# Two transposes per batch taken from TensorE, done in 32x32 squares by VectorE with a trip through DRAM

## The chip, the cores and the metric

The kernel runs on one core of one Trainium2 chip. The metric is the device time of one execution in microseconds: 476.37 us is the median of three runs (476.28, 476.37 and 478.12).

## The reference, cut to what matters

There are 8 batch entries (B = 8) of 512 rows (T) by 256 channels (D), all float32. For each entry:

```python
emb  = layernorm(x) + ctx                       # T x D
q, k, v = emb @ wq + bq, emb @ wk + bk, emb @ wv + bv
ek   = exp(k - max_over_rows(k));  ew = exp(w - max_of_row(w))   # w: T x T, a band 64 wide on each side, 0 outside
attn = (sigmoid(q) * (ew @ (ek * v)) / (ew @ ek)) @ wo + bo
a    = layernorm(attn + emb) * gamma + beta
x1   = x + tanh(g_xattn) * (layernorm(relu(a @ w1 + b1) @ w2 + b2 + a) * gamma + beta)    # hidden width 1024
xn   = layernorm(x1);  xp = xn shifted down by one row
r    = sigmoid((mu_r*xn + (1-mu_r)*xp) @ W_r.T);  kk = relu((mu_k*xn + (1-mu_k)*xp) @ W_k.T) ** 2
out  = x1 + tanh(g_ffn) * r * (kk @ W_v.T)
```

## The kernel before, in words

Every matrix product is made as three: each operand is split in a high part (rounded to TensorE's fp32r type, by ScalarE) and a low part (the rest, a subtraction on VectorE or GpSimd), and high*high, high*low and low*high are added. So almost every stage is: TensorE writes PSUM, ScalarE makes `*_hi`, VectorE or GpSimd makes `*_lo`, TensorE reads both.

Some values lie with rows on the partitions ("row form") and some with channels on the partitions ("channel form"). To turn a 512x256 array from one into the other, TensorE multiplies eight 128x128 tiles by the identity (`turn`, `turn_back`). Per entry this happens four times: the embedding (`turn_emb`), the exponentials of the keys (`turn_keys`, from `ek_t`, which is the buffer `y`, into PSUM pair 0), the normalised attention output (`turn(2, norm, mid_turned)`) and the last layer norm (`turn_fin`, from `norm` into PSUM pair 2). What follows the keys' turn is `ek_high` (ScalarE), `keys_low` and `weigh_values` (VectorE, ek * v, which gives `res`), `ev_high` (ScalarE) and `ev_low` (GpSimd). What follows the last norm's turn is `turned_copy` (ScalarE, into `xn_t`), `delta_of` (GpSimd, the difference to the row before), `mix_k` and `mix_r` (VectorE), their splits, and the products `ffn_k` and `ffn_r`.

The order on each engine is written out by hand. A prologue treats entry 0; then `step(i, p)` runs for i = 1 to 7 on every engine, and an epilogue finishes entries 6 and 7. A step works on several entries at once: i is in attention and its first hidden layers, b = i-1 in the second hidden layers and the two norms behind them, a = i-2 in the gated product at the end, d = i+1 has its keys, queries and values made, and e = i+2 is loaded. Engines wait for each other by semaphores only. TensorE's step begins with `weigh(i, 0, ...)` (ew @ ek), then `turn_emb(d)`, `weigh(i, 1, ...)` (ew @ (ek*v)) with `add_hidden(b, 1)` inside, `ffn_k(a)`, `keys(d)`, and ends with `turn(2, norm, mid_turned)`, `queries(d)`, `hidden(i, 0)`, `hidden(i, 1)`, `values(d)`, `turn_keys(d)`, `add_hidden(i, 0)`, `turn_fin(b)`. SyncE issues the DMAs of a step in the order x again, x, ctx, store.

Names in rows: PSUM is `ps`; the keys' and the ek*v parts are `ek_hi`, `ek_lo`, `ev_hi`, `ev_lo`; the buffer `res` also holds the values; `y` holds the keys' exponentials or the attention's quotient. Buffers are shared, so `ek_lo<-y,ek_hi` (line 225) on GpSimd is `y_low`, the low part of the quotient, `hid_lo<-xr,hid_hi` is `xr_low`, and `ev_lo<-xk,ev_hi` is `sq_low`.

## Time and profile before

| | |
|---|---|
| median of 3 runs | 476.37 us |
| the profiled execution's own time | 477.9 us |
| its span, first to last instruction | 476.2 us |
| TensorE busy | 453.5 us (95%), 3080 matmuls |
| VectorE busy | 391.8 us (82%), 733 instructions |
| ScalarE busy | 239.6 us (50%) |
| GpSimd busy | 259.4 us (54%) |
| DMA | 23.35 MB, 49 GB/s on average |
| granted TensorE clock, mean | 0.996 |

The span is cut in 40 slices on the page. TensorE stands at 9 tenths (90% or more) in nearly every one behind the first ten; its clock is at 9 tenths of full speed or more in all. The repeated step is read best in a stretch between two turns of the same kind. In a row of the timeline the first number is the start, the second the time from the first to the last of the merged instructions, and the bracket is idle time of the engine ahead of them with what ended it.

### The profile page before, as it was taken

How to read it: one execution, taken by the hardware profiler on the slowest of the kernel's cores; microseconds unless marked ns; L12 is line 12 of the kernel's file. 1: busy time of each engine (PE TensorE's matmuls, PEld its weight loads, DVE VectorE, ACT ScalarE, POOL GpSimd, SP SyncE). 2: the span in 40 equal slices, each digit the busy share in tenths (PEclk: the TensorE clock that was granted, in tenths of full speed). 3: DMA queues.
4: the chain of work that ended last, by engine and by line, in shares of the span. 5: the costliest groups of instructions: out<-in, count | busy, mean ns of one | idle time of the engine just before them, and what ended most of it. 6: DMA issues, size and time to landing. Idle time of an engine off the chain costs nothing.

```text
span 476.2 us, 8229 instructions
## 1 busy us (share of the span) xinstructions
PE 453.5 (95%) x3080; PEld 412.4 (87%) x3080; DVE 391.8 (82%) x733; ACT 239.6 (50%) x372; POOL 259.4 (54%) x239
## 2 busy tenths in 40 slices
PE   7889989899999999999999999999999999999975
PEld 7779788779989898999989898899989898897975
DVE  4898879986959989598968989599867979489987
ACT  3582562645265634736356643735345543538253
POOL 2574843661587535971577634973567335953621
PEclk9999999989999999999999999999999999999999
DMA  8740410102001300022001210021000110011002
GB/s 265 267 132 8 144 50 2 44 12 79 1 1 63 114 3 0 1 89 89 1 1 45 94 41 1 1 89 44 1 2 0 51 39 1 1 45 45 2 0 89
DMA packets 21895, 23.35 MB, mean 49 GB/s; under 512 B 992, under 2 KB 20960, under 8 KB 21856
## 3 DMA queue, kind: packets, MB, share of 16 engines
q1 hardware_dynamic: 20768, 21.26, 13.7%
q10 hardware_dynamic: 1088, 1.57, 1.0%
q8 instruction: 24, 0.39, 0.3%
q14 instruction: 15, 0.12, 0.1%
...
## 4 chain that ended last, share of the span: by engine, by line
PE 43%; issue 19%; POOL 16%; DVE 14%; ACT 4%; DMA 2%; ACTq 0%; POOLq 0%; DVEq 0%
PE ps L1361 40%; DVE y L670 4%; POOL xk_lo L225 3%; POOL hid_lo L225 3%; PE ps L1367 2%; POOL a_rows L434 2%; DMA hid<-in_wo 2%; DVE xk L738 1%; PE ps L1376 1%; POOL emb L434 1%; POOL ek_lo L225 1%; POOL ev_lo L225 1%; POOL x_beta L434 1%; DVE y L667 1%; DVE hid_lo L814 1%
## 5 line engine op out<-in xcount | busy, mean ns | idle before, releaser
L1361 PE MATMUL ps<-w_hi,hid_hi 128*128 128x256 f32 x288 | 72.2, 288 | 0.8 <-issue 0.5
L1361 PE MATMUL ps<-w_lo,hid_hi 128*128 128x256 f32 x288 | 70.6, 281 | 0.0
L814 DVE SCALAR_TENSOR_TENSOR hid_lo<-ps,neg_b,hid 128x512 fp32r<-128x512 f32 x60 | 41.3, 739 | 34.5 <-ACT hid L1190 34.5
L1361 PEld LDWEIGHTS ps<-w_hi,hid_hi 128*128 128x128 f32 x288 | 54.2, 188 | 3.5 <-DVE y L677 2.2
L1361 PEld LDWEIGHTS ps<-w_lo,hid_hi 128*128 128x128 f32 x288 | 54.3, 189 | 0.1
L670 DVE RECIPROCAL y<-y 128x512 f32<-128x512 f32 x16 | 53.7, 3353 | 0.6
L1361 PE MATMUL ps<-a_hi,w_hi 128*128 128x512 f32 x128 | 50.8, 397 | 1.1 <-DVE hid_lo L814 1.1
L1361 PE MATMUL ps<-a_hi,w_lo 128*128 128x512 f32 x128 | 50.7, 396 | 0.0
L1184 ACT ACTIVATE hid_hi<-ps,b 128x512 fp32r<-128x512 f32 x60 | 37.9, 686 | 24.8 <-PE ps L1361 24.8
L225 POOL TENSOR_TENSOR ev_lo<-res,ev_hi 128x1024 fp32r<-128x1024 f32 x8 | 19.1, 2383 | 51.7 <-ACT ev_hi L1129 51.7
L1361 PE MATMUL ps<-w_hi,hid_lo 128*128 128x256 f32 x288 | 41.6, 284 | 3.4 <-DVE hid_lo L814 2.2
L1361 PEld LDWEIGHTS ps<-w_hi,hid_lo 128*128 128x128 f32 x288 | 37.1, 188 | 4.8 <-DVE hid_lo L814 2.4
L1190 ACT ACTIVATE hid<-hid_hi,neg_b 128x512 f32<-128x512 f32 x60 | 40.1, 725 | 0.0
L1361 PE MATMUL ps<-a_lo,w_hi 128*128 128x512 f32 x128 | 35.1, 396 | 0.0
L434 POOL TENSOR_TENSOR a_rows<-norm,gamma_rows 128x1024 f32<-128x1024 f32 x8 | 20.1, 2509 | 19.7 <-issue 17.3
L1361 PEld LDWEIGHTS ps<-a_hi,w_hi 128*128 128x128 f32 x128 | 24.0, 188 | 6.7 <-DVE hid_lo L814 1.6
L225 POOL TENSOR_TENSOR xk_lo<-xk,xk_hi 128x1024 fp32r<-128x1024 f32 x7 | 17.2, 2460 | 22.6 <-ACT xk_hi L1141 22.6
L1361 PEld LDWEIGHTS ps<-a_lo,w_hi 128*128 128x128 f32 x128 | 24.1, 188 | 5.8
L1361 PEld LDWEIGHTS ps<-a_hi,w_lo 128*128 128x128 f32 x128 | 24.1, 189 | 5.2
L1361 PE MATMUL ps<-emb_hi,w_hi 128*128 128x512 f32 x64 | 26.9, 420 | 0.5 <-ACT emb_hi L1099 0.5
L1361 PE MATMUL ps<-emb_hi,w_lo 128*128 128x512 f32 x64 | 25.6, 399 | 0.0
L225 POOL TENSOR_TENSOR hid_lo<-xr,hid_hi 128x1024 fp32r<-128x1024 f32 x5 | 12.1, 2410 | 22.5 <-ACT hid_hi L1148 22.5
...
## 6 DMA issues: line engine op xcount, KB each, us to landing
x_in<-in_x SPq DMA_DIRECT2D x8, 512.0 KB, 4.4
emb<-in_ctx SPq DMA_DIRECT2D x8, 512.0 KB, 3.5
x_beta<-in_x SPq DMA_DIRECT2D x8, 512.0 KB, 3.6
out<-out_sb SPq DMA_DIRECT2D x7, 512.0 KB, 2.9
hid<-in_w SPq DMA_DIRECT2D x2, 512.0 KB, 6.8
x<-in_pos ACTq DMA_DIRECT2D x1, 512.0 KB, 6.2
out_sb<-in_pos ACTq DMA_DIRECT2D x1, 512.0 KB, 7.1
x<-in_w SPq DMA_DIRECT2D x1, 512.0 KB, 4.0
```

What stands on the lines that cost most here:

```text
L225: eng.tensor_tensor(dst, src, f32(hi), ALU.subtract).then_inc(done, 1)
L434: pool.tensor_tensor(dst.rearrange("p (a d) -> p a d", a=TT), src.rearrange("p (a d) -> p a d", a=TT), r, op).then_inc(done, 1)
L667: dve.scalar_tensor_tensor(out=tile(y, c, T), in0=tile(gate_q, c, T), scalar=1.0, in1=bank(1, c), op0=ALU.add, op1=ALU.mult).then_inc(den_ ...
L670: dve.reciprocal(tile(y, c, T), tile(y, c, T)).then_inc(recip_done, 1)
L738: dve.scalar_tensor_tensor(out=tile(dst, c, T), in0=tile(out_sb, c, T), scalar=vec[:, mu + c:mu + c + 1], in1=xn_t[:, c * (T + 1):c * (T + ...
L814: dve.scalar_tensor_tensor(out=tile(lo, b, T), in0=bank(relu_pair(n, q), b), scalar=neg_b1[:, m:m + 1], in1=tile(shifted, b, T), op0=ALU.m ...
L1184: act.activation(tile(hi, b, T), bank(relu_pair(n, q), b), ACT.Relu, bias=b1[:, m:m + 1]).then_inc(hid_hi_done, 1)
L1190: act.activation(tile(shifted, b, T), f32(tile(hi, b, T)), ACT.Identity, bias=neg_b1[:, m:m + 1]).then_inc(hid_shifted, 1)
L1361: return pe.matmul(o, s, m, start=start, stop=stop, skip_group_check=True)
L1367: last = pe.transpose(bank(dst, c)[:, a * P:(a + 1) * P], src[:, D * a + c * P:D * a + (c + 1) * P], ident)
L1376: last = pe.transpose(tile(pair(dst), a)[:, c * P:(c + 1) * P], src[:, T * c + a * P:T * c + (a + 1) * P], ident)
```

## The change

From entry 2 on (`FIRST_EK`) the keys, and for entries 0 to 5 the last norm, are no longer turned by TensorE. VectorE turns each 32x32 square in place among its own 32 partitions (`dve.transpose`, `turn_key_squares`, `turn_fin_squares`, two instructions of 128x512 each) into a blocks buffer (`norm` for the keys, `hid[0]` for the norm). SyncE then stores this buffer to DRAM in one DMA of 512 KB (`room`), waits for it, and reads it back in four DMAs of 128 KB, each to 32 partitions (`spread`), into `y` for the keys and `hid[1]` for the norm. The squares land in another order of columns, so the readers use views (`by_squares`, `by_columns`). The keys' low part goes from VectorE (`keys_low`) to GpSimd (`ek_low`, between the `ff` and the `fin` statistics). The values' weighing reads `y` in SBUF in place of PSUM. `recip` is cut in `gate_den` and `recip`. Orders: on TensorE `turn_emb` goes one entry ahead, to where `turn_keys` was, and `keys(d)` comes ahead of `ffn_k(a)`; on ScalarE `turned_copy` goes to the next step behind `sums_high(i, 1)`, `ek_high` comes ahead of `hidden_high(i, 0)`; on VectorE `hidden_low(i, 1)` moves behind `normalise_fin`, the squares and `keep_values`, and `emb_low` moves ahead of the first `gate_den`.

VectorE, the end of step 4, before (`res<-ps,bv_rows` is `keep_values`, `ek_lo` is `keys_low`, `res<-ps,res` is `weigh_values`; `hid_lo` x4 is both `hidden_low(i, 0)` and `(i, 1)`):

```order
L572 BN_STATS st_fin<-x 128x6 x4
L580 MEMSET held 128x1
L582 BN_AGGR mv_fin<-st_fin 128x2 x4
L814 SCALAR_TENSOR_TENSOR hid_lo<-ps,neg_b,hid 128x512 x4
L719 TENSOR_SCALAR norm<-x,rs_fin,nmr_fin 128x256 x3
L618 TENSOR_TENSOR res<-ps,bv_rows 128x1024
L637 TENSOR_TENSOR ek_lo<-ps,ek_hi 128x1024
L642 TENSOR_TENSOR res<-ps,res 128x1024
```

and now:

```order
L636 BN_STATS st_fin<-x 128x6 x4
L644 MEMSET held 128x1
L646 BN_AGGR mv_fin<-st_fin 128x2 x4
L903 SCALAR_TENSOR_TENSOR hid_lo<-ps,neg_b,hid 128x512 x2
L806 TENSOR_SCALAR norm<-x,rs_fin,nmr_fin 128x256 x3
L725 STREAM_TRANSPOSE hid<-norm 128x4x128 x2
L682 TENSOR_TENSOR res<-ps,bv_rows 128x1024
L903 SCALAR_TENSOR_TENSOR hid_lo<-ps,neg_b,hid 128x512 x2
L710 TENSOR_TENSOR res<-y,res 128x1024
```

`keys_low` has left, two square transposes stand behind the norm, and `hidden_low(i, 1)` comes later.

VectorE, the middle of step 5, ahead of the attention's sum (`res<-ps,emb`), before:

```order
L572 BN_STATS st_head<-x_in 128x6 x4
L580 MEMSET held 128x1
L582 BN_AGGR mv_head<-st_head 128x2 x4
L814 SCALAR_TENSOR_TENSOR hid_lo<-ps,neg_b,hid 128x512 x2
L626 TENSOR_REDUCE ek_sums<-y 128x4 x2
L630 COPY ek_rows<-ek_sums 128x6x4
L774 TENSOR_TENSOR res<-ps,emb 128x1024
```

and now:

```order
L636 BN_STATS st_head<-x_in 128x6 x4
L644 MEMSET held 128x1
L646 BN_AGGR mv_head<-st_head 128x2 x4
L718 STREAM_TRANSPOSE norm<-y 128x16x32 x2
L690 TENSOR_REDUCE ek_sums<-y 128x4 x2
L694 COPY ek_rows<-ek_sums 128x6x4
L903 SCALAR_TENSOR_TENSOR hid_lo<-ps,neg_b,hid 128x512 x2
L863 TENSOR_TENSOR res<-ps,emb 128x1024
```

The two square transposes of the keys read `y` and write `norm`; the keys' row sums come ahead of the low part of the hidden layer.

GpSimd, the end of step 4, before:

```order
L429 TENSOR_TENSOR nmr_ff<-nm_ff,rs_ff 128x4
L419 TENSOR_TENSOR ve_fin<-mv_fin,eps_col 128x4
L420 TENSOR_TENSOR nm_fin<-mv_fin,minus_one 128x4
L427 TENSOR_TENSOR rs_fin<-ve_fin,minus_half 128x4
L429 TENSOR_TENSOR nmr_fin<-nm_fin,rs_fin 128x4
L225 TENSOR_TENSOR ev_lo<-res,ev_hi 128x1024
```

and now:

```order
L490 TENSOR_TENSOR nmr_ff<-nm_ff,rs_ff 128x4
L231 TENSOR_TENSOR ek_lo<-y,ek_hi 128x1024
L480 TENSOR_TENSOR ve_fin<-mv_fin,eps_col 128x4
L481 TENSOR_TENSOR nm_fin<-mv_fin,minus_one 128x4
L488 TENSOR_TENSOR rs_fin<-ve_fin,minus_half 128x4
L490 TENSOR_TENSOR nmr_fin<-nm_fin,rs_fin 128x4
L231 TENSOR_TENSOR ev_lo<-res,ev_hi 128x1024
```

The keys' low part stands between the statistics `ff` and `fin` of entry b; the row `ev_lo<-res,ev_hi` is the first of the next step.

The diff, cut:

```diff
+SQ = 32
+NB = P // SQ
+FIRST_EK = 2
...
+        ek_blocks, ek_square = norm, y
+        fin_blocks, fin_square = hid[0], hid[1]
+        def by_squares(ap):
+            return ap.rearrange("p (a x j) -> p x a j", a=NB, j=SQ)
+        def by_columns(ap):
+            return ap.rearrange("p (x a j) -> p x a j", a=NB, j=SQ)
...
+        def ek_low(eng, n):
+            low(eng, by_columns(ek_lo), by_squares(ek_square), by_columns(ek_hi), ek_hi_done, n + 1, ek_lo_done)
...
+            def spread(square, blocks, room, filled, free, free_count, landed):
+                sp.dma_start(room.rearrange("(p n) -> p n", p=P), blocks).then_inc(room_filled, 16)
+                sp.wait_ge(room_filled, 16 * filled)
+                sp.wait_ge(free, free_count)
+                for b in range(NB):
+                    sp.dma_start(square[SQ * b:SQ * (b + 1)].rearrange("i (a n) -> i a n", a=NB),
+                                 room.rearrange("(a i b n) -> b i a n", a=NB, i=SQ, b=NB)[b]).then_inc(landed, 16)
+            def spread_keys(n):
+                sp.wait_ge(ek_turned, FIRST_EK + DC * (n + 1 - FIRST_EK))
+                after(sp, ek_landed, keys_moved(n - 1))
+                spread(ek_square, ek_blocks, rooms[0], keys_room(n), ek_summed, DC * (n + 1), ek_landed)
+            def spread_fin(n):
+                sp.wait_ge(fin_turned, DC * (n + 1))
+                after(sp, fin_landed, fin_moved(n - 1))
+                spread(fin_square, fin_blocks, rooms[1], fin_room(n), hid_lo_done, 2 * (NQ * (n + 1) + 2), fin_landed)
...
                     load_x(i + 2)
+                if has(i + 1):
+                    spread_keys(i + 1)
+                if has(i + 2):
                     load_ctx(i + 2, p)
                 if has(i - 2):
                     store(i - 2)
+                if not is_last(i):
+                    spread_fin(i - 1)
...
                 stats("ff", b)
+                if has(d):
+                    pool.wait_ge(x1_done, TT * (b + 1))
+                    ek_low(pool, d)
                 stats("fin", b)
...
             def weigh_values(n):
                 dve.wait_ge(val_done, n + 1)
-                dve.tensor_tensor(val, pair(0), val, ALU.mult).then_inc(ev_done, 1)
+                if n < FIRST_EK:
+                    dve.tensor_tensor(val, pair(0), val, ALU.mult).then_inc(ev_done, 1)
+                else:
+                    dve.wait_ge(ek_landed, keys_moved(n))
+                    dve.tensor_tensor(by_columns(val), by_squares(ek_square), by_columns(val), ALU.mult).then_inc(ev_done, 1)
+            def turn_key_squares(n):
+                dve.wait_ge(mid_turned, 1)
+                dve.wait_ge(a_scaled_done, 1)
+                dve.wait_ge(ek_done, DC * (n + 1))
+                for c in range(DC):
+                    dve.transpose(ek_blocks.rearrange("p (b x c i) -> p c b x i", b=NB, x=TT, c=DC)[:, c],
+                                  tile(ek_t, c, T).rearrange("p (x b i) -> p b x i", x=TT, b=NB)).then_inc(ek_turned, 1)
+            def turn_fin_squares(n):
+                dve.wait_ge(norm_done["fin"], TT * (n + 1))
+                for c in range(DC):
+                    dve.transpose(fin_blocks.rearrange("p (b c x j) -> p c b x j", b=NB, x=TT, c=DC)[:, c],
+                                  norm.rearrange("p (x c b i) -> p c b x i", c=DC, x=TT, b=NB)[:, c]).then_inc(fin_turned, 1)
...
-            def recip(n, c):
+            def gate_den(n, c):
                 dve.wait_ge(den_done, DC * n + c + 1)
                 dve.wait_ge(exp_q_done, DC * n + c + 1)
-                if c == 0:
+                if c == 0 and n < FIRST_EK:
                     dve.wait_ge(ek_turned, n + 1)
                 dve.scalar_tensor_tensor(out=tile(y, c, T), in0=tile(gate_q, c, T), scalar=1.0, in1=bank(1, c),
                                          op0=ALU.add, op1=ALU.mult).then_inc(den_read, 1)
+            def recip(n, c):
                 dve.wait_ge(den_read, DC * n + c + 1)
                 dve.reciprocal(tile(y, c, T), tile(y, c, T)).then_inc(recip_done, 1)
...
@@ -723,6 +810,8 @@
                 after(dve, fin_turned, DC * (n - 1))
                 dve.wait_ge(nmr_done["mid"], n + 1)
+                if n > 0 and has(n + 1):
+                    dve.wait_ge(room_filled, 16 * keys_room(n + 1))
                 normalise_tiles("mid", res, range(TT - FIRST_DVE, TT))
...
             def step(i, p):
                 a, b, d, e = i - 2, i - 1, i + 1, i + 2
                 sums_low(i, 0)
+                if has(d) and d > FIRST_EK:
+                    emb_low(d)
+                gate_den(i, 0)
                 recip(i, 0)
                 sums_low(i, 1)
+                gate_den(i, 1)
+                if d == FIRST_EK:
+                    emb_low(d)
                 if has(a):
                     mix_k(a)
-                if has(d):
-                    emb_low(d)
                 recip(i, 1)
                 if has(a):
...
                 if has(e):
                     head_stats(e)
+                if has(d):
+                    turn_key_squares(d)
+                    sum_keys(d)
                 hidden_low(b, 2)
-                if has(d):
-                    sum_keys(d)
                 attention_sum(i, p)
                 hidden_low(b, 3)
...
                 finish_x1(b)
                 fin_stats(b)
                 hidden_low(i, 0)
-                hidden_low(i, 1)
-                normalise_fin(b)
+                if not is_last(i):
+                    normalise_fin(b)
+                    turn_fin_squares(b)
                 if has(d):
                     keep_values(d)
-                    keys_low(d)
+                hidden_low(i, 1)
+                if is_last(i):
+                    normalise_fin(b)
+                if has(d):
                     weigh_values(d)
...
             def ek_high(n):
-                act.wait_ge(ek_turned, n + 1)
+                if n < FIRST_EK:
+                    act.wait_ge(ek_turned, n + 1)
+                    act.activation(ek_hi, pair(0), ACT.Copy).then_inc(ek_hi_done, 1)
+                else:
+                    act.wait_ge(ek_landed, keys_moved(n))
+                    act.activation(by_columns(ek_hi), by_squares(ek_square), ACT.Copy).then_inc(ek_hi_done, 1)
...
@@ -1132,8 +1238,14 @@
                 after(act, xr_done, DC * n)
                 for c in range(DC):
                     o = c * (T + 1) + 1
-                    act.wait_ge(fin_turned, DC * n + c + 1)
-                    act.activation(xn_t[:, o:o + T], bank(2, c), ACT.Copy).then_inc(xn_t_done, 1)
+                    if n == BATCH - 2:
+                        act.wait_ge(fin_turned, DC * n + c + 1)
+                        act.activation(xn_t[:, o:o + T], bank(2, c), ACT.Copy).then_inc(xn_t_done, 1)
+                    else:
+                        act.wait_ge(fin_landed, fin_moved(n))
+                        act.activation(by_columns(xn_t[:, o:o + T]),
+                                       fin_square.rearrange("p (a c x j) -> p c x a j", a=NB, c=DC, j=SQ)[:, c], ACT.Copy
+                                       ).then_inc(xn_t_done, 1)
...
             def step(i, p):
                 a, b, d, e = i - 2, i - 1, i + 1, i + 2
-                if has(d):
-                    after(act, v_done, d)
+                if d == FIRST_EK:
+                    act.wait_ge(v_done, d)
                     emb_high(d)
                 if has(a):
+                    turned_copy(a)
                     mixed_high(a)
                     mixed_r_high(a)
                     relu_k(a)
...
                 if has(d):
                     exp_q(d)
+                    ek_high(d)
                 hidden_high(i, 0)
                 hidden_high(i, 1)
                 normalise("fin", b, x1)
-                if has(d):
-                    ek_high(d)
-                if not is_last(i):
-                    turned_copy(b)
+                if has(e):
+                    act.wait_ge(v_done, e)
+                    emb_high(e)
                 if has(d):
                     sums_high(d, 0)
                     ev_high(d)
@@ -1443,7 +1556,10 @@
...
             def turn_emb(n, p):
                 pe.wait_ge(emb_done, n + 1)
-                after(pe, ev_done, n)
+                if n <= FIRST_EK:
+                    after(pe, ev_done, n)
+                else:
+                    relus_read(NQ * (n - 2) + 1)
...
                 if part == 0:
                     pe.wait_ge(lo_ready, n + 1)
                     near(dst, 0, lo, (ew_hi,))
-                    after(pe, xn_t_done, DC * (n - 1))
                     relus_read(NQ * (n - 1) + 2)
...
                 pe.wait_ge(ek_hi_done, i + 1)
                 pe.wait_ge(val_done, i + 1)
                 weigh(i, 0, 1, ek_hi, ek_lo, ek_lo_done, den_done)
-                if has(d):
+                if d == FIRST_EK:
                     turn_emb(d, 1 - p)
                 pe.wait_ge(ev_hi_done, i + 1)
                 pe.wait_ge(sums_lo_done, 2 * i + 1)
                 weigh(i, 1, 2, ev_hi, ev_lo, ev_lo_done, num_done, lambda: add_hidden(b, 1))
+                if has(d):
+                    keys(d)
                 if has(a):
                     if a == 0:
                         for u in (6, 7):
                             pe.wait_ge(w_lo_done[u], 1)
                     ffn_k(a)
-                if has(d):
...
                 hidden(i, 1)
                 if has(d):
                     values(d)
-                    turn_keys(d)
+                if has(e):
+                    turn_emb(e, p)
                 if not is_last(i):
                     add_hidden(i, 0)
-                    turn_fin(b)
```

## Rows read from the trace of the kernel before

**Rows 1.** Table of stretches: length, busy (instructions) of PE, PEld, DVE, ACT, POOL, clock, DMA.

```profile
207.60:262.00 54.40, 54.18 (x372) 49.48 (x371) 45.46 (x88) 28.11 (x43) 32.47 (x28) 1.00 0.12 40
```

**Rows 2.** Chain of waits, two steps: start, us, engine, output and line.

```profile
207.58 0.87 PE ps L1367 x8
...
219.76 0.87 PE ps L1376 x8
...
223.50 0.87 PE ps L1367 x8
...
262.03 0.87 PE ps L1367 x8
```

**Rows 3.** Timeline of PE, `weigh(4, 1)`, the first product that reads `ev_lo`.

```profile
229.88 0.63 PE L1361 MATMUL ps<-ev_lo,tile_rows 128*68 128x256 f32 x4
```

**Rows 4.** Timeline of POOL, end of step 3 and step 4.

```profile
218.12 0.20 POOL L419 TENSOR_TENSOR ve_fin<-mv_fin,eps_col 128x4 f32<-128x4 f32 x1 [3.40 <-DVE mv_fin L582]
...
219.64 0.20 POOL L429 TENSOR_TENSOR nmr_fin<-nm_fin,rs_fin 128x4 f32<-128x4 f32 x1
227.40 2.38 POOL L225 TENSOR_TENSOR ev_lo<-res,ev_hi 128x1024 fp32r<-128x1024 f32 x1 [7.56 <-ACT ev_hi L1129]
229.73 2.04 POOL L259 TENSOR_TENSOR out_sb<-xn_t 128x512 f32<-128x512 f32 x2
...
245.97 2.39 POOL L225 TENSOR_TENSOR ek_lo<-y,ek_hi 128x1024 fp32r<-128x1024 f32 x1
...
250.00 2.40 POOL L225 TENSOR_TENSOR ev_lo<-xk,ev_hi 128x1024 fp32r<-128x1024 f32 x1
```

**Rows 5.** Timeline of DVE, the same stretch.

```profile
214.49 1.71 DVE L696 SCALAR_TENSOR_TENSOR x<-x,rs_ff,x_beta 128x256 f32<-128x256 f32 x4 [0.52 <-POOL rs_ff L427]
...
220.57 1.05 DVE L719 TENSOR_SCALAR norm<-x,rs_fin,nmr_fin 128x256 f32<-128x256 f32 x3
...
223.80 1.22 DVE L642 TENSOR_TENSOR res<-ps,res 128x1024 f32<-128x1024 f32 x1
...
232.17 1.42 DVE L738 SCALAR_TENSOR_TENSOR xk<-out_sb,vec,xn_t 128x512 f32<-128x512 f32 x2
...
238.74 1.32 DVE L738 SCALAR_TENSOR_TENSOR xr<-out_sb,vec,xn_t 128x512 f32<-128x512 f32 x2
...
251.59 1.41 DVE L814 SCALAR_TENSOR_TENSOR hid_lo<-ps,neg_b,hid 128x512 fp32r<-128x512 f32 x2 [4.92 <-ACT hid L1190]
...
254.72 1.21 DVE L774 TENSOR_TENSOR res<-ps,emb 128x1024 f32<-128x1024 f32 x1
```

**Rows 6.** Timeline of ACT, the same stretch.

```profile
226.27 1.05 ACT L1129 ACTIVATE ev_hi<-res 128x1024 fp32r<-128x1024 f32 x1
...
248.46 1.26 ACT L1105 ACTIVATE y<-ps,kbias 128x512 f32<-128x512 f32 x2 [2.48 <-POOL ek_lo L225]
```

**Rows 7.** Timeline of DVE, end of step 1.

```profile
103.65 1.71 DVE L696 SCALAR_TENSOR_TENSOR x<-x,rs_ff,x_beta 128x256 f32<-128x256 f32 x4
...
114.56 1.21 DVE L642 TENSOR_TENSOR res<-ps,res 128x1024 f32<-128x1024 f32 x1
```

**Rows 8.** Timeline of DVE and POOL where both ran at once, in two places.

```profile
81.09 2.40 POOL L225 TENSOR_TENSOR ek_lo<-y,ek_hi 128x1024 fp32r<-128x1024 f32 x1 [7.49 <-ACT ek_hi L1166]
...
81.65 2.93 DVE L653 TENSOR_TENSOR w_lo<-x,w_hi 128x1024 fp32r<-128x1024 f32 x1
```

```profile
434.18 2.41 POOL L434 TENSOR_TENSOR x_beta<-x_beta,beta_t 128x1024 f32<-128x1024 f32 x1
...
434.91 2.47 DVE L719 TENSOR_SCALAR norm<-x,rs_fin,nmr_fin 128x256 f32<-128x256 f32 x3
```

**Rows 9.** Groups by line: the reciprocal; busy, mean ns, idle before.

```profile
L670 DVE RECIPROCAL y<-y 128x512 f32<-128x512 f32 x16 | 53.7, 3353 | 0.6
```

**Rows 10.** DMA issues by line: engine, count, KB each, us to landing.

```profile
emb<-in_ctx SPq DMA_DIRECT2D x8, 512.0 KB, 3.5
...
out<-out_sb SPq DMA_DIRECT2D x7, 512.0 KB, 2.9
```

More of the change, by code:

```diff
@@ L200, in flamingo_gated_block @@
         gated_done, out_done = sem("gated_done"), sem("out_done")
+        ek_landed, fin_landed = sem("ek_landed"), sem("fin_landed")
+        room_filled = sem("room_filled")
+        rooms = [nc.dram_tensor(f"room{k}", [P * PAIR], F32, kind="Internal").ap() for k in range(2)]
         last_norm_dve, last_sq_lo = sem("last_norm_dve"), sem("last_sq_lo")
@@ L1082, in normalise @@
                 act.wait_ge(nmr_done[kind], n + 1)
+                if kind == "mid" and n > 0 and has(n + 1):
+                    act.wait_ge(room_filled, 16 * keys_room(n + 1))
                 for a in range(FIN_DVE if kind == "fin" else 0, TT - FIRST_DVE if kind == "mid" else TT):
@@ L1709, in step @@
                     ffn_k(a)
-                if has(d):
-                    keys(d)
                 if is_last(i):
```

13 lines of the change are left out of this document (11 added, 2 removed).

## The prediction

> **What bounds the kernel now.** I read the table of stretches first: in a stretch of 54.40 us TensorE is busy for 54.18, VectorE for 45.46, GpSimd for 32.47 [rows 1]. The chain of waits gives the period: the turn behind the middle norm stands at 207.58 and again at 262.03, so a step takes 54.45 us, and each turn of eight tiles is 0.87 us of the path [rows 2]. TensorE sets the pace. Then I looked how far the others are behind, because TensorE gives way only as far as they let it. GpSimd ends `ev_lo` at 227.40 + 2.38 = 229.78, and TensorE takes it up at 229.88 [rows 3, 4]: 0.1 us of slack. VectorE's only long idle time in a step is 4.92 us, ahead of `hidden_low(b, 2)` [rows 5]. So the kernel is at two bounds at once, TensorE's work and a ring of VectorE, ScalarE and GpSimd.
>
> **What TensorE saves.** Steps 1 to 6 lose one `turn_keys` and one `turn_fin` each: 12 x 0.87 = 10.4 us [rows 2]. `turn_emb` only moves. If TensorE alone decided, that would be the gain.
>
> **The ring behind the change.** I follow it from w, the end of `weigh_values`, to the next w. Before, w = 223.80 + 1.22 = 225.02, and it comes back after 54.45.
>
> 1. w to `ev_lo`. `ev_high` is 1.05 [rows 6], `ev_low` 2.38 [rows 4], with hand-overs w + 3.55. Before it took 4.76, since `ev_high` stood behind `sums_high`.
> 2. `turned_copy(a)` now stands behind `sums_high(i, 1)`, which needs four products that read `ev_lo`. I take 1.6 for these, the copy of the sums and the first half of `turned_copy`: 0.5 for the products (merged row 0.63, rows 3), two times half of a 1.05 copy [rows 6]. `delta_of` takes 2.04 [rows 4]; `mix_k` reads its result: w + 7.2. `mix_k` 1.42 [rows 5]: w + 8.65. Until then VectorE does `emb_low`, both gate products and the first reciprocal, which hides them. The second reciprocal 3.35 [rows 9], `mix_r` 1.32: w + 13.3. Before, `mix_r` ended at 238.74 + 1.32 = 240.06, w + 15.04 [rows 5].
> 3. From there to `exp_keys` the same chain as before: 248.46 - 240.06 = 8.4 [rows 5, 6], w + 21.7.
> 4. `exp_keys` 1.26 [rows 6]. Then the two squares of the keys, 1.35 (below), the row sums and their copy, 254.72 - 253.00 = 1.7, `hidden_low(b, 2)` 1.41 [rows 5]: the attention's sum starts at w + 27.45. Before: 254.72, w + 29.7. The squares use up part of the 4.92 of idle time.
> 5. From the attention's sum to the end of `finish_x1`: 214.49 + 1.71 + 54.45 - 254.72 = 15.9, unchanged: w + 43.4.
> 6. From there to the next w. Before 225.02 - 216.20 = 8.8. Now GpSimd does `ek_low` first, 2.4 as for any 128x1024 row of its kind, and VectorE's statistics (1.9, ended by 218.12) hide only part of it. The four small operations 219.84 - 218.12 = 1.7 [rows 4], the norm's three tiles 1.05, squares 1.35, `keep_values` 1.22 (priced as `weigh_values`), `hidden_low(i, 1)` 1.41, `weigh_values` 1.22, less 0.3 for overlapping neighbours [rows 5]: 10.25. `keys_low` (1.2) has left; the squares and the wait for GpSimd eat more than that.
>
> Sum 43.4 + 10.25 = 53.65, against 54.45: 0.8 us per step, not the 1.74 that TensorE would allow. TensorE will wait about 1.1 us per step for `ev_lo`, and for `val_done` some tenths.
>
> **The sum.** In step 1 the stretch from `finish_x1` to w was 115.77 - 105.36 = 10.4 [rows 7], already as long as the new 10.25, so w stays at 115.6. In step 2 `ev_high` still stands behind `sums_high`; I add 0.95 for that. The last changed end is that of step 6: 115.6 + 0.95 + 5 x 53.65 = 384.8, `ev_lo` at 388.35. Before, TensorE took it at 229.88 + 3 x 54.45 = 393.23. The gain is 4.9 us. Step 7 and the epilogue have the same work. The profiled execution took 477.9 (span 476.2), so it would take 473.0; the median of the runs lies 1.5 lower, at 476.37, and I forecast 471.5.
>
> **What the trace doesn't show.** A square transpose. The lower end is a plain instruction of the same size, half of 1.32, so 0.66 [rows 5]; the upper end is the slowest of that size, 3.35 [rows 9]. I take 0.67: the data moves once, nothing is iterated. Each further 0.1 costs 0.1 x 4 x 5 = 2 us in all, since all four of a step lie on the ring. At the upper end the kernel would take 54 us more; I give that no weight worth a range. Views with a column order of 32 in ScalarE's, GpSimd's and VectorE's readers: between no cost and, for five instructions of 1 to 2.4 us, a doubling of some; I take nothing.
>
> The trip through DRAM. A store of 512 KB lands in 2.9, a load of 512 KB in 3.5 [rows 10]: 6.4 as the lower end; one load after another, 2.9 + 4 x 3.5 = 16.9 as the upper. The four are issued without a wait between, so I add 1.2 for their issues: 7.6. For the norm the time from the squares' end (w - 3.65) to `turned_copy` (w + 4.6) is 8.25: hidden, with 0.6 to spare, and every microsecond beyond that is one more per step. At the upper end it would be 8.6 x 5 = 43 us. The keys have 15 us, from w + 24.35 to `ek_high` near w + 40: hidden. Behind the norm's trip on SyncE's queue wait the next `load_again` and `load_x`; their data is wanted 14 us later. Behind the keys' trip waits `load_ctx`, which before went out right after the attention's sum; it is wanted by GpSimd 9 us later and lands in 3.5.
>
> **Ports.** At 81.65 a VectorE instruction with two SBUF inputs took 2.93 us; a GpSimd one ran from 81.09 to 83.49, and the first ended 1.1 after it. At 434.91 three norm tiles took 2.47 in place of 1.05, beside GpSimd's 434.18 to 436.59 [rows 5, 8]. So some VectorE instructions wait until GpSimd's is done. `weigh_values` now has two SBUF inputs, but GpSimd is idle there; `mix_k` has two, and I have let it start only behind `delta_of`. Whether a square transpose waits no row shows. The Trainium skill (SBUF — State Buffer, Who interferes with whom) says that a VectorE instruction with at most one SBUF input and outside the two-port modes does not contend with GpSimd, and names `tensor_scalar`, which the second pair of rows shows waiting, among those that do. By that rule the trace agrees for both pairs, and the transposes would not wait.
>
> **The rivals.** *TensorE decides alone* (all 10.4 us are gained): 466.0. For it: the ring is only 0.8 us shorter by sums of rows, and an error of 0.2 on each of six hand-overs would open it. Against it: `ev_lo` was already just in time [rows 3, 4] and `ek_low` now delays the statistics.
>
> *The trip or the views take the gain away*: the norm lands 1 us late per step, 5 x 1.0 = 5, giving 476.5. For it: a DMA that waits in SyncE's queue for `hid_lo_done` and issues four parts has only 0.6 to spare. Against it: DMA is lightly loaded, busy for 0.12 [rows 1].
>
> *The squares cost more than a plain instruction*: place, the four of VectorE on the ring; price, 20 us in all per microsecond of one. It decides for slower from 0.67 + (4.9 + 2.4) / 20 = 1.03 us on. At twice the plain time, 0.67 more, it gives 471.5 + 13.4 = 485. Nothing in the rows speaks for it but the reciprocal, which has the same shape and takes 5 times as long.
>
> The Trainium skill (VectorE: DVE Perf Modes, The three transpose paths) gives VectorE 311 ns for a 128x128 block of bf16 and in its rules names TensorE for full tiles; eight such blocks would be an estimate of 2.5 us where I have 1.35, and the time by that 483. No row here shows it, and the page's figure holds the fixed part of one small instruction.
>
> *The keys' squares wait for GpSimd*, as `tensor_scalar` does in rows 8. `y_low` ends at w + 21.7 as before at 248.36, the head's statistics last until 250.00, and there `sq_low` takes 2.40 [rows 4]: from w + 23.4 to 25.8. The second square would start at 23.7 and wait 2.1. Five steps: 10.5 more, 482.
>
> **How the numbers follow.** Less than 0.5% (2.4 us) cannot be told from no change. The forecast, the ring at about 53.65 per step: 0.46, with its own range 468.5 to 474.0. TensorE alone: 0.13. The trip or the views: 0.17. Dear squares: 0.12. Squares that wait: 0.12. Faster: 0.46 + 0.13 = 0.59; same: 0.17; slower: 0.24. The range reaches from a little below TensorE's bound, 465.5, to 482, where the waiting squares lie; the dear ones are left out.
>
> **What will show it.** In the profile after: a turn of the middle norm every 53.6 to 53.7 us; TensorE idle for about 1 us per step ahead of the product that reads `ev_lo`; two squares in 1.3 to 1.4 us, at both places; the ring's stretch from `finish_x1` to w 10.2 long; ScalarE's `turned_copy` started by `sums_high` and not by a DMA. I am wrong if `turned_copy` waits for the landing, if a square takes over 1 us, if VectorE waits for something new inside the ring, or if the period is 52.7 (TensorE alone).

## The result: slower by 1.4%, where a gain of 1% was forecast

| | before | after |
|---|---|---|
| median | 476.32 us (4 runs, 475.46 to 478.12) | 483.07 us (4 runs, 481.24 to 486.18) |
| ratio, 95% interval | | 1.014 (1.008 to 1.021) |
| the profiled execution's own time, span | 477.9, 476.2 us | 481.24, 479.5 us |
| TensorE, VectorE, GpSimd busy | 453.5, 391.8, 259.4 us | 444.7, 402.6, 273.0 us |
| DMA | 23.35 MB | 35.95 MB |

The forecast was 471.5. The runs after are also further apart than those before, and their times follow the clock: granted clocks of 0.996, 0.991, 0.988 and 0.984 go with 481.24, 481.9, 484.24 and 486.18 us. Of the six runs of e2 below, the three that were over 1.5% above its fastest (489.05 to 490.7 us, clocks of 0.983 to 0.988) count as slow and are left out of its numbers.

The page of the changed kernel shows that the change did what it says. TensorE has 96 instructions fewer and 8.8 us less to do, and the trips are there (engine, times, KB each, us to landing):

```profile
PE 444.7 (93%) x2984; PEld 402.6 (84%) x2984; DVE 402.6 (84%) x751; ACT 238.9 (50%) x372; POOL 273.0 (57%) x245
...
room<-norm SPq DMA_DIRECT2D x6, 512.0 KB, 2.7
y<-room SPq DMA_DIRECT2D x24, 128.0 KB, 2.9
room<-hid SPq DMA_DIRECT2D x6, 512.0 KB, 2.7
hid<-room SPq DMA_DIRECT2D x24, 128.0 KB, 3.0
```

The table of stretches, each from one attention sum to the next, is the profile after's answer to [rows 1]:

```profile
142.66:198.63 55.97, 52.46 (x354) 47.88 (x354) 48.42 (x90) 30.14 (x48) 36.88 (x31) 1.00 0.25 80
198.63:254.33 55.70, 54.27 (x354) 49.33 (x354) 46.77 (x90) 25.85 (x40) 32.32 (x29) 0.97 0.22 72
254.33:310.30 55.97, 52.46 (x354) 47.88 (x354) 48.49 (x90) 30.14 (x48) 36.89 (x31) 1.00 0.26 81
310.30:364.60 54.30, 52.46 (x354) 47.88 (x354) 45.07 (x82) 24.90 (x38) 33.09 (x26) 1.00 0.20 64
```

TensorE's work per step is down from 54.18 to 52.46 us, as forecast. But the steps are not alike: 55.97, 55.70, 55.97, 54.30, where before each took 54.45 and the forecast had 53.65. Something costs 2.3 us in some steps and nothing in others. VectorE's timeline has it (in rows, L718 and L725 are the squares, L694 the copy that spreads the keys' row sums, L863 the attention's sum, L710 `weigh_values`):

```profile
168.16 1.22 DVE L710 TENSOR_TENSOR res<-y,res 128x1024 f32<-128x1024 f32 x1
...
194.97 2.43 DVE L694 COPY ek_rows<-ek_sums 128x24 f32<-128x24 f32 x1
...
198.63 1.21 DVE L863 TENSOR_TENSOR res<-ps,emb 128x1024 f32<-128x1024 f32 x1
...
208.88 1.29 DVE L792 TENSOR_TENSOR res<-ps,a_rows 128x512 f32<-128x512 f32 x2 [2.31 <-PE ps L1474]
...
215.73 0.87 DVE L783 SCALAR_TENSOR_TENSOR x<-x,rs_ff,x_beta 128x256 f32<-128x256 f32 x2
...
221.99 1.30 DVE L725 STREAM_TRANSPOSE hid<-norm 128x512 f32<-128x512 f32 x2
...
225.63 1.22 DVE L710 TENSOR_TENSOR res<-y,res 128x1024 f32<-128x1024 f32 x1
...
250.42 1.30 DVE L718 STREAM_TRANSPOSE norm<-y 128x512 f32<-128x512 f32 x2 [2.66 <-ACT y L1207]
251.65 1.24 DVE L690 TENSOR_REDUCE ek_sums<-y 128x4 f32<-128x512 f32 x2
252.92 0.18 DVE L694 COPY ek_rows<-ek_sums 128x24 f32<-128x24 f32 x1
253.01 1.40 DVE L903 SCALAR_TENSOR_TENSOR hid_lo<-ps,neg_b,hid 128x512 fp32r<-128x512 f32 x2
254.33 1.21 DVE L863 TENSOR_TENSOR res<-ps,emb 128x1024 f32<-128x1024 f32 x1
...
306.63 2.43 DVE L694 COPY ek_rows<-ek_sums 128x24 f32<-128x24 f32 x1
```

The same copy of 24 numbers per partition takes 2.43 us, then 0.18, then 2.43. GpSimd's timeline at the second and third of them:

```profile
250.56 2.42 POOL L231 TENSOR_TENSOR ev_lo<-xk,ev_hi 128x1024 fp32r<-128x1024 f32 x1
...
252.94 2.42 POOL L495 TENSOR_TENSOR a_rows<-a_rows,bias_rows 128x1024 f32<-128x1024 f32 x1
...
304.27 2.43 POOL L231 TENSOR_TENSOR ev_lo<-xk,ev_hi 128x1024 fp32r<-128x1024 f32 x1
...
306.64 2.39 POOL L495 TENSOR_TENSOR a_rows<-a_rows,bias_rows 128x1024 f32<-128x1024 f32 x1
```

The copy that starts at 306.63 comes while `sq_low` ends and `a_rows` begins; it is over when `a_rows` is, at 309.03. The one at 252.92 came 0.06 us before `sq_low`'s end and 0.02 before `a_rows`, and got through. The one at 141.25 got through as well (0.18 us), though it came 0.07 before `sq_low`'s end and 0.01 before `a_rows`, just like the one at 306.63: which of the two happens is decided below the hundredth of a microsecond that the profile prints. Behind the copy stands `hidden_low(b, 2)`, and TensorE's `ffn_v` waits for that:

```profile
198.86 0.36 PE L1474 MATMUL ps<-w_hi,ev_hi 128*128 128x256 f32 x1 [2.87 <-DVE hid_lo L903]
...
230.62 0.69 PE L1474 MATMUL ps<-ev_lo,tile_rows 128*68 128x256 f32 x4 [0.64 <-POOL ev_lo L231]
...
254.56 0.36 PE L1474 MATMUL ps<-w_hi,ev_hi 128*128 128x256 f32 x1 [0.59 <-DVE hid_lo L903]
...
310.53 0.36 PE L1474 MATMUL ps<-w_hi,ev_hi 128*128 128x256 f32 x1 [2.87 <-DVE hid_lo L903]
```

The first of the two waits of 2.87 us had a second cost. Stretches of the table (columns as above; the clock is the last number but two):

```profile
196.00:200.10 4.10, 1.24 (x8) 1.27 (x9) 4.07 (x5) 3.04 (x6) 3.69 (x2) 0.92 0.45 132
200.10:204.20 4.10, 4.10 (x26) 4.10 (x25) 3.55 (x12) 0.61 (x2) 1.57 (x4) 0.66 0.38 128
...
308.00:312.00 4.00, 1.47 (x12) 1.50 (x13) 3.96 (x6) 2.70 (x5) 3.36 (x2) 1.00 0.46 131
312.00:316.00 4.00, 4.00 (x36) 4.00 (x35) 3.96 (x12) 0.75 (x2) 1.57 (x4) 1.00 0.47 135
```

TensorE was busy for 1.24 of 4.10 us, and in the stretch behind it the granted clock averages 0.66, that is 1.2 GHz for about two thirds of it and 2.4 GHz for the rest. That makes 1.5 of the 2.0 us by which the step of 55.70 is longer than one of 53.7, although its own copy took only 0.18 us. TensorE's 354 instructions of that step take 54.27 us in place of 52.46, VectorE waits 2.31 us for `ff_sum` (`res<-ps,a_rows`, 208.88) where it waits 1.42 in the other steps, and from the attention's sum to the end of `finish_x1` it is 17.98 us in place of 16.47. Most of the rest, 0.4 us, is ScalarE's `turned_copy`, which waits in this step for the norm's trip to land:

```profile
232.13 1.16 ACT L1246 ACTIVATE xn_t<-hid 128x512 f32<-128x512 f32 x2 [0.40 <-DMA hid<-room]
```

Behind the second wait, as long and with TensorE busy for 1.47 of 4.00, the clock stayed at 2.4 GHz. The runs with lower mean clocks, above, are the longer ones.

### The profile page after: what moved, and what is told of

The parts are those of the page before. It is cut to its first block, busy times and chain, and to the rows that moved or that the text cites. A ratio compares the mean times of both kernels' runs of the same rounds, so it can differ in the third digit from the quotient of the medians.

```text
span 479.5 us, 8151 instructions
## 1 busy us (share of the span) xinstructions
PE 444.7 (93%) x2984; PEld 402.6 (84%) x2984; DVE 402.6 (84%) x751; ACT 238.9 (50%) x372; POOL 273.0 (57%) x245
## 2 busy tenths in 40 slices
DMA packets 30536, 35.95 MB, mean 75 GB/s; under 512 B 1952, under 2 KB 28064, under 8 KB 30496
## 4 chain that ended last, share of the span: by engine, by line
PE 30%; POOL 21%; DVE 20%; issue 20%; ACT 5%; DMA 2%; SPq 0%; DVEq 0%; POOLq 0%; ACTq 0%
PE ps L1474 28%; POOL ek_lo L231 4%; POOL xk_lo L231 3%; DVE y L757 3%; POOL hid_lo L231 2%; POOL emb L495 2%; POOL a_rows L495 2%; DVE hid_lo L903 2%; DVE xk L827 2%; PE ps L1480 2%; DVE emb_lo L654 2%; DVE y L751 1%; DVE ek_sums L690 1%; ACT y L1207 1%; POOL x_beta L495 1%
## 5 line engine op out<-in xcount | busy, mean ns | idle before, releaser
L1474 PEld LDWEIGHTS ps<-w_lo,hid_hi 128*128 128x128 f32 x288 | 54.4, 189 | 0.2
L757 DVE RECIPROCAL y<-y 128x512 f32<-128x512 f32 x16 | 53.5, 3347 | 0.3
L231 POOL TENSOR_TENSOR ek_lo<-y,ek_hi 128x1024 fp32r<-128x1024 f32 x13 | 31.2, 2400 | 16.6 <-DVE x L783 9.2
L1230 ACT ACTIVATE sums_r<-ps 68x256 fp32r<-68x256 f32 x16 | 6.1, 380 | 43.7 <-PE ps L1607 23.5
```

The lines of the kernel that those rows point to most:

```text
L231: eng.tensor_tensor(dst, src, f32(hi), ALU.subtract).then_inc(done, 1)
L757: dve.reciprocal(tile(y, c, T), tile(y, c, T)).then_inc(recip_done, 1)
L1230: act.activation(sums_r[part][0:FAR], bank(2, part, D)[0:FAR], ACT.Copy).then_inc(sums_hi_done, 1)
L1474: return pe.matmul(o, s, m, start=start, stop=stop, skip_group_check=True)
```

## The experiments

Theory: the copy waits for GpSimd's running instruction, and the 2.4 us of that wait, together with what stands behind it, turn a gain into a loss. Rivals: moving the data through DRAM, or the new orders, cost it. In each batch of runs, before ran on the same chip (476.83, 476.78 and 476.62 us); the changed kernel as it stands was measured only with the result above, where before took 476.32.

**e1: the copy as a reduction.** The same numbers in the same place, as a `tensor_reduce` over an axis of length 1.

```diff
-dve.tensor_copy(ek_rows..., ek_sums...)
+dve.tensor_reduce(ek_rows..., ek_sums... (last axis of length 1), AX_X, ALU.add)
```

> The changed kernel, with the small copy of the keys' row sums (ek_rows, 128x24) made by a tensor_reduce over an axis of length one in place of tensor_copy. Theory (the copy waits until a GpSimd instruction is done, 2.43 us in place of 0.18 in steps 3 and 5, and TensorE's ffn_v behind it): no copy above 0.4 us, TensorE's wait ahead of ffn_v 0.6 us in every step in place of 2.87 in two, the ring at 54.2 us per step, 474.5 us, and less scatter. Rival (the trips through DRAM and the longer ring make the loss, the two waits are hidden by others): within 1 us of the changed kernel's 481 to 486.

Measured 472.69 us (472.16 to 474.44), ratio 0.992 (0.990 to 0.994). One instruction in another form takes 10.4 us off the changed kernel (483.07), and makes the change a gain of 0.8%. The theory held, and by more than it promised. Every such instruction takes 0.18 us, and the steps of the loop are alike:

```profile
142.20:195.91 53.71, 52.46 (x354) 47.88 (x354) 46.16 (x90) 27.87 (x44) 34.61 (x30) 1.00 0.26 79
195.91:249.65 53.74, 52.47 (x354) 47.89 (x354) 46.17 (x91) 27.89 (x44) 34.62 (x30) 1.00 0.25 79
249.65:303.37 53.72, 52.46 (x354) 47.88 (x354) 46.24 (x90) 27.88 (x44) 34.59 (x30) 1.00 0.25 79
```

**e10: the copy stays, GpSimd waits.** This tells the form of the instruction from the wait: `tensor_copy` in its place, and GpSimd's `a_rows` held back until it is done.

```diff
+                if has(d):
+                    pool.wait_ge(ek_rows_done, d + 1)
                 finish_a(b, 1 - p)
                 x_plus_beta(b)
```

> The changed kernel with tensor_copy kept in its form and its place; GpSimd alone is edited: it waits for the row sums' copy before it starts a_rows (and so x_beta behind it). Theory (the copy waits for whatever GpSimd instruction runs, and missed the gap between two of them by hundredths of a us): the copies of 2.43 us become 0.2 to 0.3, at most what is left of ev_lo, no TensorE wait of 2.87 ahead of ffn_v, time 472 to 475. Rival (the copy's form is dear by itself, whatever GpSimd does): copies stay at 1.8 to 2.4 us and the time at 481 or more.

Measured 473.62 (472.42 to 475.72), ratio 0.994 (0.992 to 0.997), as the theory had it. The timeline, VectorE and GpSimd together:

```profile
246.06 2.41 POOL L231 TENSOR_TENSOR ev_lo<-xk,ev_hi 128x1024 fp32r<-128x1024 f32 x1
...
248.42 0.18 DVE L696 COPY ek_rows<-ek_sums 128x24 f32<-128x24 f32 x1
...
248.68 2.39 POOL L495 TENSOR_TENSOR a_rows<-a_rows,bias_rows 128x1024 f32<-128x1024 f32 x1 [0.20 <-DVE ek_rows L696]
```

The copy takes 0.18 us in steps 1 to 6, and a step 53.71 to 53.73. So the form is not dear by itself; what costs is GpSimd's instruction beside it. This is the decisive run, since VectorE's program is untouched. Below I call this wait, of a VectorE instruction for the end of GpSimd's, the lock. Span against span the changed kernel loses 479.5 - 472.1 = 7.4 us to it. The attention's sums of the two kernels show where: 1.5 us by the first (a copy of 1.79), 0.3 by the second (1.3 given back), then 2.2, 2.0, 2.3 and 0.6 more.

**e2 and e6: the keys alone**, the last norm turned by TensorE as before, with `turned_copy` and VectorE's end of the step in their old places; e6 with the reduction.

```diff
-                    spread_fin(i - 1)
-                    turn_fin_squares(b)
+                    turn_fin(b)        # TensorE, with turned_copy from PSUM
```

> Only the keys turned in squares; the last norm is turned by TensorE as before, and VectorE's end of the step stands in the old order without keys_low. Theory (each part is paid in VectorE's ring): TensorE saves 5.2 us; the stretch from finish_x1 to the end of weigh_values is about 8 us, so the ring would allow 53 us, but the keys' squares and the copy's wait delay hidden_low(b, 2) and ffn_v behind it, in some steps by 2.4: 473 to 477 us. Rival (the norm's part is what loses, the keys' part gains): 471 or less.

> The keys-only half of the change (last norm turned by TensorE as before) with the row-sum copy as tensor_reduce. Theory (the two copies of 2.43 to 2.44 us and the two TensorE waits of 2.56 behind them made keys-only slow): those waits shrink to about 0.6, time 473 to 477, scatter between runs under 3 us. Rival (moving the keys through DRAM is what costs, by its trips or its place on the queues): 483 or more with no copy over 0.2 us.

Measured for e2 482.68 (479.61 to 483.32), ratio 1.010 (1.006 to 1.014). Both the theory and the rival missed. The theory had the copy's wait in it, but priced it too low: it is 2.43 us in two steps and 1.80 in an earlier one, and the clock comes on top. The copy waits in two steps one after the other, and TensorE with it:

```profile
196.60 2.44 DVE L692 COPY ek_rows<-ek_sums 128x24 f32<-128x24 f32 x1
...
253.16 2.43 DVE L692 COPY ek_rows<-ek_sums 128x24 f32<-128x24 f32 x1
```

```profile
200.50 0.36 PE L1468 MATMUL ps<-w_hi,ev_hi 128*128 128x256 f32 x1 [2.56 <-DVE hid_lo L901]
...
257.05 0.55 PE L1468 MATMUL ps<-w_hi,ev_hi 128*128 128x256 f32 x1 [2.57 <-DVE hid_lo L901]
```

Behind the second of these waits the granted clock was 0.58 over 4.10 us; behind the first it stayed at 1.00, although TensorE had been busy for 1.94 of the 4.00 us before the one and for 1.98 of the 4.20 before the other. Span against span e2 loses 481.0 - 472.0 = 9.0 us to e6. With the reduction, e6: 474.12 (473.58 to 476.38), ratio 0.995 (0.993 to 0.997), as the theory had it. The two waits are 0.33 us. No engine waits for the landing of the keys in e6 or in the changed kernel, so the keys' trip through DRAM costs nothing that can be seen.

**e3: the last norm alone**, keys turned by TensorE as before, `keys_low` back on VectorE behind the norm's squares. The orders that the change had brought for the keys are undone too: `emb_low` and the second gate product stand behind `mix_k` again, `hidden_low(b, 2)` ahead of the row sums.

> Only the last norm turned in squares; keys as before, with keys_low on VectorE, hidden_low(b, 2) ahead of the row sums as before. Theory: the stretch from finish_x1 to the end of weigh_values grows from 8.8 to about 10.7, and emb_low and the gate products are again behind mix_k, so the ring is longer than 54.45 by 1 to 2 us although TensorE saves 0.87 per step: 479 to 484 us. Rival (the keys' part loses, by the copy's wait): faster than before by some of the 5.2 us, 472 to 475.

Measured 488.53 (488.01 to 488.6), ratio 1.024 (1.022 to 1.027). Slower, and by more than expected, but not by the copy, which stands behind `hidden_low(b, 2)` there and takes 0.58 to 0.60 as before. A step takes 56.7 us, 2.2 more than before. Of these, 2.1 lie between `finish_x1`'s end and w (10.9 against 8.8), where the squares and `keys_low` now both stand ahead of `weigh_values`. TensorE waits there for `ek_lo`, which comes later than before:

```profile
228.51 0.70 PE L1460 MATMUL ps<-ew_hi,ek_lo 128*128 128x192 f32 x4 [1.21 <-DVE ek_lo L696]
```

That does not show that the norm's half pays only without `keys_low`. Beside e1, where a step takes 53.7, only 0.6 us of the 3.0 more lie between `finish_x1` and w. Another 2.9 lie between w and the attention's sum (29.9 against 27.0), where the second reciprocal starts 10.6 us behind w in place of 8.7, behind `emb_low` and the gate product; 0.5 are given back behind the sum. The norm's squares with the new order and the keys on TensorE were not run. With both halves and the reduction (e1) the norm's half is worth 474.12 - 472.69 = 1.4 us more by the medians, but the intervals of the two ratios overlap.

**e5: the reduction in the kernel before**, as a control.

> The kernel before with one edit: the copy that spreads the keys' row sums (128x24) is written as a tensor_reduce over an axis of length 1. In the before trace that copy took 0.58 us in most steps and 1.67 and 1.26 in two, with VectorE's next work close behind it. Theory (the copy waits for GpSimd's running instruction, and before had almost none running there): copies of 0.18, gain 0.4 us a step in the ring, 2 to 3 us in all: 473.5 to 475. Rival (tensor_reduce helps for some other reason, as by a shorter instruction as such, so that it would gain in before what it gained in the changed kernel, some 10 us): 466 to 468.

Measured 474.95 (474.8 to 476.39), ratio 0.997 (0.996 to 0.998): in the range expected, and about a sixth of what the same edit brings to the changed kernel (1.8 of 10.4 us). The way there was not the theory's. A step still takes 54.43 us (54.45 before), with TensorE's work of 54.18 in it. Of the 1.7 us between the two profiled spans, 1.05 lie ahead of step 1 already (the first attention sum starts at 43.06 and 44.11); the profiled executions of the other kernels fall on one or the other of these starts as well. The other 0.7 are what is left at the end of 1.5 gained in step 1, where the copy had taken 1.67. The control sent me back to two rows of before that I had not read, GpSimd's and VectorE's:

```profile
252.37 2.40 POOL L434 TENSOR_TENSOR a_rows<-a_rows,bias_rows 128x1024 f32<-128x1024 f32 x1
...
254.22 0.58 DVE L630 COPY ek_rows<-ek_sums 128x24 f32<-128x24 f32 x1
```

The copy of 0.58 us ended at 254.80, just behind `a_rows` at 254.77. It was waiting there already, for the last 0.4 us, at no cost to the step.

**e7 and e8: another place.** `hidden_low(b, 2)` goes between the squares and the row sums; e7 keeps the copy, e8 has the reduction.

```diff
                 turn_key_squares(d)
+                hidden_low(b, 2)
                 sum_keys(d)
-                hidden_low(b, 2)
```

> The changed kernel with tensor_copy kept, but hidden_low(b,2) moved ahead of sum_keys (squares, hidden_low, sums, copy). TensorE's ffn_v no longer waits behind the copy, but the attention sum does. The copy would start near where GpSimd has 0.4 to 1.0 us of a_rows or x_beta left, so it still waits some. Theory (the copy's wait is charged to whoever stands behind it): no TensorE wait of 2.87 ahead of ffn_v, copies of 0.5 to 2.4 us, time 473 to 479. Rival (the wait is only harmful in VectorE's own chain, not through ffn_v): no better than the changed kernel, 481 or more.

> As the one before, with the row-sum copy as tensor_reduce. Beside e1 (472.7) it takes away the 0.6 us that TensorE still waits ahead of ffn_v, at the price that hidden_low may wait 0.4 us for ScalarE ahead of the sums. Theory of the ring (w to attention sum sets the step, TensorE has slack): within 1 us of e1, 471.7 to 473.7. Rival (TensorE's own waits set the step in e1): gains 0.6 us in each of five steps, 469.5 to 470.5.

Measured for e7 475.4 (474.72 to 476.9), ratio 0.997 (0.996 to 0.999); for e8 471.79 (471.67 to 472.87), ratio 0.990 (0.987 to 0.992). In e7 the copy is late enough to meet only the end of `a_rows`:

```profile
249.35 2.41 POOL L495 TENSOR_TENSOR a_rows<-a_rows,bias_rows 128x1024 f32<-128x1024 f32 x1
...
251.20 0.60 DVE L694 COPY ek_rows<-ek_sums 128x24 f32<-128x24 f32 x1
```

The theory held: with this order alone the change is 0.3% faster than before. e8 is 0.9 us faster than e1 by the medians, but their ranges overlap. TensorE's wait of 0.6 us ahead of `ffn_v` is gone in it, and with it VectorE's wait for `ff_sum`: from the attention's sum to the end of `finish_x1` it is 15.93 us in place of 16.47. But from w to the sum it is 27.47 in place of 27.01, because `hidden_low(b, 2)` waits 0.44 for ScalarE, so a step takes 53.66 to 53.72, as in e1. One step takes 54.87. In it the norm's trip was late, 9.4 us from the squares' end:

```profile
173.86 1.16 ACT L1247 ACTIVATE xn_t<-hid 128x512 f32<-128x512 f32 x2 [1.12 <-DMA hid<-room]
```

**e4 and e11: the same lock at another instruction.** In e4 (with the reduction) GpSimd's `ek_low` goes behind the last norm's statistics, so that VectorE waits for them less. In e11 it also waits until the norm is made.

```diff
-                if has(d):
-                    pool.wait_ge(x1_done, TT * (b + 1))
-                    ek_low(pool, d)
                 stats("fin", b)
+                if has(d):
+                    pool.wait_ge(norm_done["fin"], TT * (b + 1))   # e11 only
+                    ek_low(pool, d)
```

> As e1_reduce, and GpSimd makes the keys' low part behind the statistics of the last norm in place of ahead of them. Theory (VectorE's idle time of 1.14 ahead of norm is on the ring in every step): that idle time goes, 5 to 6 us less than e1_reduce, about 469 us. Rival (TensorE's wait for hidden_low(b, 2) ahead of ffn_v sets the pace): no gain over e1_reduce beyond 1 us.

> e4 with one more wait: GpSimd's ek_low (2.4 us) stands behind the last norm's statistics and also waits until the norm has been made. Beside e4 (481.5, where VectorE's three norm tiles took 2.99 us beside GpSimd's ek_lo, against 1.06 in e1). Theory (e4 lost by the same lock, on another one-source instruction): norm tiles 1.06 us, VectorE's wait for nmr_fin 0.64 in place of 1.15, time 470 to 473. Rival (ek_low is late for TensorE's weigh, and that cost e4 its time): 478 or more, with norm tiles of 1.06.

e4: 481.53 (480.35 to 483.24), ratio 1.010 (1.007 to 1.013). Both my theory and its rival missed; it is 8.8 us slower than e1, and a step takes 55.0. Three norm tiles that need 1.06 us take 2.99: the first waits for the end of `ek_lo` at 221.74, the others follow.

```profile
219.36 2.38 POOL L231 TENSOR_TENSOR ek_lo<-y,ek_hi 128x1024 fp32r<-128x1024 f32 x1
219.55 2.99 DVE L805 TENSOR_SCALAR norm<-x,rs_fin,nmr_fin 128x256 f32<-128x256 f32 x3 [0.64 <-POOL nmr_fin L490]
```

e11: 471.95 (471.44 to 473.52), ratio 0.991 (0.988 to 0.995), as the theory had it. With `ek_low` even later, the tiles are back at 1.06:

```profile
214.58 1.06 DVE L806 TENSOR_SCALAR norm<-x,rs_fin,nmr_fin 128x256 f32<-128x256 f32 x3 [0.64 <-POOL nmr_fin L490]
...
215.81 2.41 POOL L231 TENSOR_TENSOR ek_lo<-y,ek_hi 128x1024 fp32r<-128x1024 f32 x1 [1.36 <-ACT norm L1169]
```

So e4 lost by the lock and not by a late `ek_lo`. The 0.5 us less of waiting for `nmr_fin` brought the step nothing (53.71): VectorE waits longer further on instead, 0.76 in place of 0.34 us ahead of `sums_low`.

**e9 and e12: on from e8.** e9: `hidden_low(i, 0)`, `keep_values`, norm and squares, `weigh_values`, `hidden_low(i, 1)`. e12: both `hidden_low`, norm and squares, `keep_values`, `weigh_values`.

> e8 (471.8) with keep_values ahead of the norm and its squares and weigh_values straight behind the squares, hidden_low(i,1) last. VectorE's 1.14 us wait for nmr_fin is partly filled, w ends 1.4 to 1.6 us earlier after the statistics, the last norm's squares leave 0.7 us later. Theory (the ring from w bounds the step, the trip of the squares has 0.65 us of slack and then delays mix_k): 0.4 to 0.9 us a step less, 467 to 470. Rival (the trip is what is late: mix_k moves by all of 0.7 us, nothing is gained): 471 to 473.

> e8 with hidden_low(i,1) ahead of the norm and its squares, then keep_values and weigh_values. VectorE's 1.14 us wait is filled by 1.4 us of work, the squares leave 0.5 us later, keep_values ends 0.6 us later or 0.8 earlier. TensorE's weigh(i,0) waits for keep_values (0.29 in e8): that wait would grow to 0.9. Theory (ring): w 0.6 us earlier, 469 to 471. Rival (TensorE's wait for keep_values decides, as it shows in e4): 472 to 476.

e9: 477.47 (474.36 to 478.93), ratio 1.002 (0.999 to 1.004); theory and rival both missed. `weigh_values` is indeed early, w stands 8.54 us behind `finish_x1` in place of 10.25, but from w to the attention's sum it is 29.5 to 29.9 in place of 27.5, and a step takes 54.0 to 54.4. `hidden_low(i, 1)`, now last, is what is late:

```profile
220.41 1.31 DVE L725 STREAM_TRANSPOSE hid<-norm 128x512 f32<-128x512 f32 x2
221.63 1.19 DVE L710 TENSOR_TENSOR res<-y,res 128x1024 f32<-128x1024 f32 x1
```

```profile
224.20 0.41 PE L1608 MATMUL ps<-ident,ek_rows 128*68 128x128 f32 x2 [0.95 <-DVE hid_lo L903]
```

```profile
224.93 1.05 ACT L1236 ACTIVATE ev_hi<-res 128x1024 fp32r<-128x1024 f32 x1
```

TensorE waits for it in the middle of `weigh(i, 0)`, in every step; ScalarE's `sums_high(d, 0)` waits for that product, and `ev_high` stands behind it, 2.11 us behind w in place of 0.03 in e8. The norm's trip is on the way in three of six steps, where `turned_copy` waits for it (1.09, 0.25 and 0.44 us). How the loss against e8 divides between the two I did not test. e12: 473.36 (470.8 to 474.82), ratio 0.992 (0.989 to 0.996), in the range of its rival; steps of 53.5 to 53.7, and a wait of 1.24 us for `keep_values` in the last one. Nothing tried beats e8, e11 and e1 by more than the scatter. All three beat both kernels.

## Why the prediction was wrong

The failed step is step 4 of the ring, in the term "the row sums and their copy, 254.72 - 253.00 = 1.7". It took a duration from a place where the copy met the last 0.4 us of `a_rows` to a place 1.9 us earlier against GpSimd (from 1.85 us behind `a_rows`' start to 0.01 or 0.02 ahead of it), where it can meet all of it. Of 1.7, 1.24 is the sums; the copy is 0.18 when GpSimd is out of its way and 2.43 when not. The paragraph on ports had the mechanism, had GpSimd's `sq_low` from w + 23.4 to 25.8, and asked only whether the squares would wait. By its own numbers the squares end near w + 24.3 and the sums at w + 25.5, so the copy falls 0.3 us ahead of the hand-over from `sq_low` to `a_rows`. In the runs it fell 0.01 or 0.02 ahead of `a_rows`, where it either slips in or waits 2.4 us, on differences too small for the profile to print. The Trainium skill (SBUF — State Buffer, Who interferes with whom) names `copy` beside `tensor_scalar` among what can contend with GpSimd, and says that `tensor_reduce` on trn2 never does; the runs agree: 2.43 and 2.99 us for the first two beside a GpSimd instruction (0.18 and 1.06 without), 0.18 in every step for the reduction.

A second step failed with it: I never asked who waits for `hidden_low(b, 2)`, which the change puts behind squares, sums and copy. It is TensorE's `ffn_v`, 0.6 us in every step and 2.87 with the locked copy. Through it VectorE waits for `ff_sum`, so from the attention's sum to `finish_x1`'s end it is 16.5 us (195.91 to 212.38 in e1), not 15.9; in e8, without that wait, it is 15.93.

Point by point, the rest:

- TensorE saves 1.74 us per step: 54.18 to 52.46 [rows 1]. Right.
- The ring, not TensorE, sets the step. Right: with the lock gone, e1, e10 and e11 have steps of 53.71 to 53.74 with 52.46 of work for TensorE, against a forecast of 53.65. In e1 the three stretches are 27.0, 16.5 and 10.3, against 27.45, 15.9 and 10.25; the first two miss by half a microsecond in opposite directions, and that they cancel is luck. As far as `exp_keys` the chain was right: w + 21.70 (222.64 to 244.34 in e1), against 21.7.
- A square costs 0.67: measured 0.65, two in 1.30, and it doesn't wait for GpSimd. *Dear squares* and *squares that wait* are out. The second had the mechanism that decided, but at the wrong instruction; that its 482 was near the result is luck.
- The trip is hidden with 0.6 us to spare: the room was right (8.2 to 8.4 us from the squares' end to `turned_copy` in e1, against 8.25), the trip's 7.6 too small. Where `turned_copy` waited for the landing, it came 8.84 and 9.09 us behind the squares' end in the changed kernel (waits of 0.40 at 232.13 and 0.81 in the last step), 8.63 once in e1, and 8.88 and 9.40 in e8. Four loads are issued over 1.7 to 2.3 us, where 1.2 were added for them. So one of the prediction's own signs of being wrong came true, at a price of some tenths in single steps. *The trip eats the gain* is out, since e1 keeps the trips.
- The views with a column order of 32: no cost to be seen. `weigh_values` takes 1.22, `ek_lo` 2.4.
- TensorE waits for `ev_lo` "about 1.1 us": 0.64, and 0.62 for `hidden_low`.
- The sum: 471.5 for a ring without the lock; e1 took 472.69. The waits behind the copy, with the clock they cost, are the other 10.4.

The clock is a term that the forecast had not at all, though before has such a stretch too: from 95.20 to 107.10 its granted clock is 0.86, so one of its slices stands at 8 tenths, and what was said of it above, 9 or more in all, is not so. In the four runs of the changed kernel it went from 0.996 to 0.984, and the time rose by 4.9 us with it. In e1 it stayed at 0.995 to 1.000. What remains open is why a TensorE wait of 2.87 us was followed by 1.2 GHz once and not the other time, and how much of the median's 10.4 us is clock: in the profiled run it is about 1.5.
